# Attention stage: softmax denominators inverted in a 128 by 16 shape reached by small transfers, with the order of stores, scatters and sums changed

## The reference

```python
qkv = x @ Wqkv                       # 16 heads of 32
k, v = compress(k), compress(v)      # 4 tokens to 1: 512 keys a batch, and one null key and value before them
dots = einsum('bhid,bhjd->bhij', q, k) * d ** -0.5     # masked: only blocks of 4 tokens that lie behind the query
attn = softmax(dots)                 # over keys: exp(dots - max) / sum
out  = einsum('bhij,bhjd->bhid', attn, v)
out  = out @ W_out + b_out
out  = fft(fft(out, axis=-1), axis=-2).real
```

## Time and profile before

| | us |
|---|---|
| median of 3 runs | 5415.87 |
| lowest, highest | 5412.05, 5418.78 |
| span of the profiled execution (first to last instruction) | 5418.5 |
| attention stage in it | about 750 to 2455 |
| TensorE's mean granted clock | 0.992 |

### The profile page before, as it was taken

The page is one execution under the profiler, slowest core; times in us unless marked ns, Lnnn a source line. Parts: engine busy times, 40 slices in busy tenths (PEclk is TensorE's granted clock), DMA queues, the critical chain, the costliest instruction groups (busy, mean ns, idle before and its releaser), DMA issues. The chain is left out here.

```text
span 5418.5 us, 102292 instructions
## 1 busy us (share of the span) xinstructions
PE 5303.0 (98%) x32880; PEld 4440.9 (82%) x32880; DVE 3828.9 (71%) x7311; ACT 2615.1 (48%) x3833; POOL 3028.9 (56%) x2716
## 2 busy tenths in 40 slices
PE   8999989999999999998999999999999999999999
PEld 6888866766666667667999999989999999999786
DVE  6666667778787877775676666766667666666664
ACT  3333333333343333335666666666666666666410
POOL 1222215666666665115777777777777777777514
PEclk9999989999999999998999999999999999999999
DMA  7777764444454444435676677767787676676748
GB/s 239 248 242 255 250 173 129 133 134 119 136 148 135 119 141 118 134 98 119 134 158 112 134 170 150 163 132 167 158 227 158 135 164 129 134 156 113 178 154 289
DMA packets 500414, 864.75 MB, mean 160 GB/s; under 512 B 64388, under 2 KB 165493, under 8 KB 497694
## 3 DMA queue, kind: packets, MB, share of 16 engines
q1 hardware_dynamic: 356014, 567.12, 33.2%
q0 software_dynamic: 140928, 292.13, 29.5%
q10 hardware_dynamic: 3312, 3.47, 0.3%
HBM read 498.49 MB, written 330.47 MB: 153 GB/s over the span
## 5 line engine op out<-in xcount | busy, mean ns | idle before, releaser
L1754 POOL DMA_INDIRECT mid_base<-e_rows,e_ox x556 | 1160.3, 2087 | 372.5 <-POOL e_ox L1749 239.5
L1865 DVE TENSOR_TENSOR e_wgu_lo<-e_wgu,e_wgu_hi 128x2048 fp32r<-128x2048 f32 x278 | 637.5, 2293 | 806.4 <-ACT e_wgu_hi L1788 676.6
L1742 POOL DMA_INDIRECT e_xg<-mid_xn,e_ix x556 | 625.5, 1125 | 336.4 <-POOL e_ix L1739 226.4
L1801 ACT CAST e_xT_hi<-e_ps_t 128x512 fp32r<-128x512 f32 x556 | 299.1, 590 | 929.8 <-PE e_ps_t L1931 929.8
L1069 POOL DMA_INDIRECT mid_ids<-b_pairs,b_cell x512 | 614.3, 1200 | 141.8 <-issue 141.0
L1944 PE MATMUL e_ps_g<-e_xT_hi,e_wgu_hi 128*128 128x256 f32 x2224 | 652.9, 294 | 1.7 <-issue 1.7
L1944 PE MATMUL e_ps_g<-e_xT_lo,e_wgu_hi 128*128 128x256 f32 x2224 | 630.0, 283 | 0.0
L1944 PE MATMUL e_ps_g<-e_xT_hi,e_wgu_lo 128*128 128x256 f32 x2224 | 629.7, 283 | 0.0
L1944 PE MATMUL e_ps_u<-e_xT_hi,e_wgu_hi 128*128 128x256 f32 x2224 | 629.4, 283 | 0.0
L1944 PE MATMUL e_ps_u<-e_xT_lo,e_wgu_hi 128*128 128x256 f32 x2224 | 629.4, 283 | 0.0
L1944 PE MATMUL e_ps_u<-e_xT_hi,e_wgu_lo 128*128 128x256 f32 x2224 | 629.4, 283 | 0.0
(11 more groups left out here) (286 smaller groups left out, 13368.0 us busy)
## 6 DMA issues: line engine op xcount, KB each, us to landing
b_xT_hi<-mid_xT_hi SPq DMA_DIRECT2D x32, 1024.0 KB
b_xT_lo<-mid_xT_lo SPq DMA_DIRECT2D x32, 1024.0 KB
mid_base<-b_x SPq DMA_DIRECT2D x32, 1024.0 KB
e_wgu<-in_gate_w SPq DMA_DIRECT2D x62, 512.0 KB
e_wgu<-in_up_w SPq DMA_DIRECT2D x62, 512.0 KB
e_wd<-in_down_w SPq DMA_DIRECT2D x62, 512.0 KB
ec_cell<-mid_base SPq DMA_DIRECT2D x88, 256.0 KB, 4.9
ab_q<-mid_q_hi SPq DMA_DIRECT2D x82, 256.0 KB, 4.0
```

Of the source, the lines that this page charges most:

```text
L1742: pool.indirect_dma_start(xg[s][:, i, :], None, t["xn"], bass.IndirectOffsetOnAxis(ap=ix[s][:, i:i + 1], axis=0))\
L1754: pool.indirect_dma_start(t[f"base{i}"], bass.IndirectOffsetOnAxis(ap=ox[s][:, i:i + 1], axis=0), rows[s][:, i, :], None, compute_op=ALU.a ...
L1801: act.copy(xT_hi[s][:, i * DC // 2 * RB:(i + 1) * DC // 2 * RB], ps_t[i][:, :]).then_inc(xT_hi_ready, 1)
L1865: dve.tensor_tensor(wgu_lo[s][:, :], wgu[s][:, :], wgu_hi[s][:, :].bitcast(F32), ALU.subtract)\
```

## The change

The 128 by 512 in-place reciprocal, done in four parts, is replaced by a chain. ScalarE issues a transfer (slot 2) that takes one partition of each head from `den` (4 rows of 512) and lays them out as 128 by 16 in `den16`. VectorE inverts that in slot 4. ScalarE issues a store of it to DRAM (slot 5) and a load (slot 7) that repeats each head's row on 32 partitions of a new tile `rden`. GpSimd's `finish` reads `rden`. SyncE issues `store_att` behind `load_x`, `load_xT` and the weight loads; GpSimd puts eight scatters ahead of `finish`; the sums over past blocks move from slots 6 and 6, 8 to slot 7 (n = 1) and 8, 9 (n = 2), and stay at 6, 8, 10 for n = 3. The last unit inverts 128 by 512 in four parts as before. In the diff, in this order: the tiles and `ADDS`; SyncE's loop over u; GpSimd's `finish` and scatters; ScalarE's three transfers and the slots in which they stand, behind the exponentials of the slot; VectorE.

```diff
+        den16 = sb("den16", [P, QC // DH])
+        rden = sb("rden", [P, QC])
...
+        ADDS = {0: (), 1: (7,), 2: (8, 9), 3: (6, 8, 10)}
...
-                if u:
-                    store_att(u - 1)
                 if gate and s:
                     load_x(s)
...
                 if u in (NU // 2 - 2, NU // 2 - 1):
                     load_raw(2 * u - NU + 12)
                     load_raw(2 * u - NU + 13)
+                if u:
+                    store_att(u - 1)
...
             def finish(u):
-                pool.wait_ge(rden_ready, QTC * (u + 1))
+                pool.wait_ge(rden_in, 16 * (u + 1))
                 pool.wait_ge(od_emptied, u + 1)
                 if u >= 2:
                     pool.wait_ge(att_out[u % 2], 16 * (u // 2))
-                pool.tensor_tensor(att[u % 2][:, :], o[:, :], den[:, :], ALU.mult).then_inc(att_ready, 1)
+                pool.tensor_tensor(att[u % 2][:, :], o[:, :], rden[:, :], ALU.mult).then_inc(att_ready, 1)
...
-                for i in mine[:4]:
+                for i in mine[:8]:
                     scatter(g, i)
                 if u:
                     finish(u - 1)
-                for i in mine[4:]:
+                for i in mine[8:]:
                     scatter(g, i)
...
+            def turn_den(u):
+                act.wait_ge(den_ready, u + 1)
+                act.dma_start(den16[:, :], den[0:P:DH, :].rearrange("h (j c) -> h j c", j=DH)).then_inc(den16_in, 16)
+
+            def store_rden(u):
+                act.wait_ge(den16_ready, u + 1)
+                act.dma_start(t["rden"].rearrange("h (j c) -> (h j) c", j=DH), den16[:, :]).then_inc(rden_out, 16)
+
+            def spread_rden(u):
+                act.wait_ge(rden_out, 16 * (u + 1))
+                if u:
+                    act.wait_ge(att_ready, u)
+                act.dma_start(rden[:, :], t["rden"][:, None, :].broadcast_to([HPC, DH, QC])).then_inc(rden_in, 16)
...
+                    if u and k == 2:
+                        turn_den(u - 1)
+                    if u and k == 5:
+                        store_rden(u - 1)
+                    if u and k == 7:
+                        spread_rden(u - 1)
...
                 if u:
                     dve.wait_ge(att_ready, u)
+                    dve.wait_ge(den16_in, 16 * u)
                 dve.tensor_tensor(den[:, :], ps_d[:, :], p_null[:, :], ALU.add).then_inc(den_ready, 1)
...
-            def invert(u, i):
-                dve.wait_ge(den_ready, u + 1)
-                part = den[:, i * P:(i + 1) * P]
-                dve.reciprocal(part, part).then_inc(rden_ready, 1)
+            def invert(u):
+                dve.wait_ge(den16_in, 16 * (u + 1))
+                dve.reciprocal(den16[:, :], den16[:, :]).then_inc(den16_ready, 1)
...
-                    if 2 <= k < QTC + 2 and u:
-                        invert(u - 1, k - 2)
+                    if k == 4 and u:
+                        invert(u - 1)
...
-                    if k in (6, 8, 10) and (k - 6) // 2 < u % NCH:
-                        add_past(u, (k - 6) // 2)
+                    if k in ADDS[u % NCH]:
+                        add_past(u, ADDS[u % NCH].index(k))
...
             normalise(NU - 1)
+            dve.wait_ge(den_ready, NU)
             for i in range(QTC):
-                invert(NU - 1, i)
+                dve.reciprocal(rden[:, i * P:(i + 1) * P], den[:, i * P:(i + 1) * P]).then_inc(rden_in, 16 // QTC)
```

More of the change, by code:

```diff
@@ L837, in stage_b @@
         od_emptied = sem("od_emptied")
-        rden_ready = sem("rden_ready")
+        den16_in = sem("den16_in")
+        den16_ready = sem("den16_ready")
+        rden_out = sem("rden_out")
+        rden_in = sem("rden_in")
         att_ready = sem("att_ready")
@@ L2322, in internal @@
         cnt=d("cnt", (P, EXPERTS)), ids=d("ids", (NSLOT, 2), I32), blk=d("blk", (1, 3 * P), I32), used=d("used", (1, 3), I32),
-        attT=d("attT", (DC, P, TOK)), passed=nc.alloc_semaphore("passed"))
+        attT=d("attT", (DC, P, TOK)), rden=d("rden", (HPC, QC)), passed=nc.alloc_semaphore("passed"))
 def layout(L0_attn_x, L0_attn_Wqkv, L0_attn_conv_w, L0_attn_conv_b, L0_attn_null_k, L0_attn_null_v, L0_attn_W_out,
```

## The result

The changed kernel takes 5431.49 us (median of 11 runs, 5424.78 to 5440.41), the kernel before, run beside it, 5417.14 (11 runs, 5412.05 to 5422.48). The ratio is 1.0027, with a 95% interval of 1.0018 to 1.0035: 14 us slower, where 51 us faster was forecast. It lies above the predicted range.

The account below looks back on a forecast made before the run. The prediction took TensorE, busy 98% of the span, as the bound. Gains of 53 us less charges of 2 made 51 us off 5415.9, so 5365 us; own range 5340 to 5390 (chance 0.60), outer ends 5332 and 5412.

Parts of the forecast that it names:

- What bounds the kernel: TensorE, busy 98% of the span; VectorE costs it 48.0 us in 127 waits of weight loads.
- the reciprocals: VectorE, attention stage: four of 0.945 us a unit become one of 0.2; 53 of 62 us of TensorE's delays go.
- the landing of `turn_den`: First small transfer, behind slot 2's exponential: lands 2.5 us from issue; burst delays together some 3 us, taken as 2.
- break-even of 4.5: `invert` in slot 4: a landing up to 4.5 us behind issue makes VectorE's score 8 no later than before.
- the third rival: VectorE stops at `invert`, slot 4, for a landing at 7 us: 5466; chance 0.15 together with one other rival.
- The sums: Sums moved to later VectorE slots: operations behind them are covered, 0 charged; without cover up to 37 us.
- `finish`: GpSimd, unit 29: load lands at 1527.2, product ends 1528.5; 2.6 us slack before the next mask, no cost.
- Order on SyncE and of the scatters: `store_att` behind row loads gains nothing, 0; eight scatters take 11.8 us, with `finish` still inside its slack.
- Issue from ScalarE: Three issues a unit, up to 3.3 us, fit between the exponentials: 0 charged, at most 57 us.
- Four engines, the second rival: Transfers out of four rows use four of 16 engines, 2.6 us more in a burst: 5378; chance 0.15.
- the sign of being wrong: VectorE idle at `invert` a microsecond or more in most units, or exponentials held behind `store_rden` or `spread_rden`.

Follow-up runs that it names:

- experiment 8: The kernel before with each of the four reciprocals over only 16 of its 128 columns, no transfers added: 5371.96 us, ratio 0.9909.
- experiment 9: The kernel before with reciprocals over only 16 of each 128 columns and the changed kernel's slots for the sums: 5375.61 us, ratio 0.992.
- experiments 5: The changed kernel with small reciprocal in slot 6, its store in 7, load in 9, and n = 2 sums back in slots 6 and 8: 5384.96 us.
- 2: The changed kernel with the sums of n = 2 put back in slots 6 and 8: 5404.55 us, ratio 0.9977.
- 3: The changed kernel with the small reciprocal in slot 6, its store in slot 7 and its load in slot 9: 5394.73 us, ratio 0.9964.
- experiment 10: The changed kernel with four scatters ahead of `finish` again instead of eight: 5434.98 us, ratio 1.003.
- 7: The kernel before with only the order changed: `store_att` behind the row loads, eight scatters ahead of `finish`: 5436.98 us, ratio 1.0029.
- 11: The changed kernel with `store_att` back ahead of `load_x` and `load_xT` on SyncE: 5631.08 us, ratio 1.039.
- experiment 12: The kernel of experiments 5 with `spread_rden` split into four transfers of 32 partitions, each from one row: 5379.77 us, ratio 0.9925.

## Why the prediction was wrong, point by point

**What bounds the kernel, and the reciprocals: right.** 53 us were expected from the relief and 48 came (experiment 8, with four reciprocals of 245 ns left in it). The small reciprocal takes 0.25 us against 0.2. VectorE's busy time fell by 141 us on the page, not by 226. The reciprocals themselves account for 223 (242 gone, 16 for the small ones, 4 for the last unit). Of the 81 us between, 35 are a matter of counting: rows that overlap their neighbours are counted once in the busy time, and 35 us less of them overlap in the changed kernel. Some 27 us are operations that got longer beside `finish`: 12.7 in L1237, 5.6 in L1232, 3.7 and 2.2 in their neighbours, 2.9 in the second sum; against them `hT_lo` got 12.5 us shorter. The row maxima's operations took 15 us longer and those of the last stage 13; why is not traced.

**The step that failed: the landing of `turn_den`.** The prediction took 2.5 us for it, with a break-even of 4.5, and charged "the 16 units of n = 0, which load keys as well: 16 x 0.1". Its delays summed to "some 3 us", of which it charged 2 without a reason. It measured 6.4 us from issue to reciprocal in n = 0 (10.63 - 4.25) and 4.4 in n = 2. Without bulk ahead the 2.5 was about right: in n = 3 the last packet is through 1.5 us after the issue and the reciprocal starts 2.6 after it. Set against experiment 8, which has the reciprocals' relief and no transfers, n = 0 units are 1.85 us longer: 16 x 1.85 = 30 us, where 1.6 was charged. The bulk was in the earlier trace rows, a DMA share of 1.07 at 1489; it was priced as a delay of one microsecond, and the trace shows that the small transfer's first packet waits until what was issued ahead of it is nearly through (in unit 36 behind 1.35 MB). The nearest row for that was ScalarE's 9.8 us in the earlier trace rows, which the third rival used and the sum did not.

**The sums: 0 was charged, and they cost up to 20 us.** n = 2 units are 1.62 us longer than in experiment 8, 26 us. Putting the sums back returns 1.24 of it (20 us), of which the sums by themselves are 0.24 (experiment 9). The prediction looked for what stands behind the sums and named `down_out` and `negate`. It missed `hT_lo` and `gate_out` behind them, which releases the gate matmuls that stand just ahead of the next unit's first scores. Nor did it ask what else runs at the new hour of `finish`, which makes the chain 0.9 us longer in each n = 2 unit. The landing's part in n = 2 is 0.36 to 0.63 us (experiments 5 against 2, and 3). In n = 1, 0.31 us is left, 5 us. 30 + 5 + 26 + 1 (n = 3) = 62 us of charges against 48 of gain: the 14 us of the result.

**`finish`: its slack was reckoned against the wrong neighbour.** It was placed at 1527.2, 18.8 us into unit 29, and called harmless because the next mask and `normalise` come later. By n it starts 19.5 to 23.4 us into the unit, where it was 11.7 to 13.7 before, so the place was nearly right, and neither the mask nor `normalise` is delayed. But it and VectorE's operations on SBUF tensors stretch each other, and what stands beside it pays.

**Order on SyncE and of the scatters: 0, right in the sum and wrong in the reason.** Undone within the change, the scatters are worth nothing (experiment 10). In the kernel before, both together cost 17 us (7). Within the change the order on SyncE keeps off the 196 us that the late `finish` would cost (11). The order on SyncE was not tried alone on the kernel before.

**Issue from ScalarE: right for TensorE.** The three issues took 0.54, 0.32 and 0.55 us, not 1.11. The exponentials are not held up, but in 12 of the n = 0 units `store_rden` holds the next activation of the gate for 26.3 us together, since it waits for the late reciprocal. No wait of TensorE is put on ScalarE.

**The rivals.** The third, VectorE stopped at the small transfer, is what happened, with the right place and a size of 16 units, not 63 (7 us assumed, 6.4 measured in n = 0). It was thought unlikely because an SBUF copy in the earlier trace rows took 2.0 us, but that is a median, of copies with little ahead of them: in the microsecond before their issue the DMA share was 0.37 on average. The 14 of the 256 copies in the kernel before that were issued at a share above 0.8 landed after 4.7 us on average, so the trace of before had the price. VectorE stood idle at `invert` in 28 of 63 units, and for a microsecond or more in 18: the sign of being wrong, "in most units", asked for more than it took. Four engines, the second rival, fits what the queue shows: each unit adds 24 packets of 4 bytes to it, with experiment 12's four loads 84. In unit 36 four of them go with the small transfer, sixteen with the store and four with the load. If each engine that takes part sends one such packet, the rule that the prediction cited from the Trainium skill ("DMA: Bandwidth & Descriptors", Rules for kernel authors) holds here. Unloaded it does not decide the time: the small transfer is through in 0.32 us. Whether the first packet would wait less in a burst if the small transfer ran on all 16 was not tried.

## What to carry to other kernels

Price a small transfer by what its issue finds in the queues, not by its size: read the DMA share at the moment of issue, take for the landing the time at which that burst ends, and put the consumer behind it or the burst behind the transfer (two slots of delay were worth 36 us here). When an operation moves to a new hour, list what each engine that shares something with it does at that hour, and not only who waits for it. When several edits come together, test each part on both kernels: the sums of n = 2 cost 4 us alone and 20 in company.

## What the runs showed of the hardware

A small transfer of 128 pieces of 64 bytes, SBUF to SBUF, has its first packet 1.19 us after the start of its issue and its last 0.32 us later when nothing is ahead; behind loads and a store issued 3 to 5 us before it from SyncE, on another queue, the first packet came after 4.41 us, and behind a 1 MB load issued 1 us before it after 3.20. The Trainium skill ("DMA: Bandwidth & Descriptors", Queues, rings and completion order) has each DMA engine take turns between queues, packet by packet. By that the small transfer would pass within a few packets of the bulk; this case's trace does not show that in n = 0 and n = 2. Packets of GpSimd's scatters, on a third queue, do move in between: 21 of them in the microsecond from 1712, while the small transfer waited. What holds back ScalarE's transfer alone stays open.

VectorE operations with two SBUF inputs are stretched by GpSimd's product of two SBUF tensors: 128 by 2048 from 2.29 to 3.19 us, 128 by 16 from 0.17 to 1.22, and GpSimd's own from 1.29 to 2.77 beside them. The Trainium skill ("SBUF — State Buffer", Who interferes with whom) states this pair as an exclusive lock for the whole instruction. The trace agrees: in unit 34 the 128 by 16 operation ends at 1670.87 and `finish` at 1670.84. Copies with one input were stretched as well: in unit 46 of the changed kernel the 128 by 16 cast inside `negate` took 1.26 us instead of 0.17. `hT_lo`, which `finish` met before the change, fell from 792 ns to 695 on average when it moved away.

A reciprocal's time is not proportional to its columns: 128 by 128 took 945 ns, 128 by 16 took 245 to 250.
